# Cross attention with layer norm: the mask folded into keys and values, the softmax maximum taken from the score banks, and the splits of x on GpSimd

## The chip, the cores and the metric

The kernel runs on one core of one Trainium2 chip. The metric is the device time of one launch in microseconds; a median of three runs is given for the kernel before. The engines are TensorE (PE in the rows, its weight loads PEld), VectorE (DVE), ScalarE (ACT), GpSimd (POOL) and SyncE (SP), whose queue issues all DMAs of this kernel. They work through their own instruction lists in order and wait for each other by semaphores.

## What is computed

```python
qh = split(q @ wq.T + bq); kh = split(k @ wk.T + bk); vh = split(v @ wv.T + bv)
scores = einsum('ntd,nsd->nts', qh, kh) / sqrt(depth)
scores = scores + repeat(mask, h, axis=0)[:, None, :] * PAD      # PAD = -2**32 + 1
ctx = einsum('nts,nsd->ntd', softmax(scores), vh)
out = merge(ctx) + q
out = (out - mean) / sqrt(var + 1e-5) * gamma + beta
```

q is x (32 x 512 x 512), k and v are the context (32 x 77 x 512), all float32; there are 16 heads of depth 32. The mask is (32, 77). The repetition over heads pairs batch and head so that a head of a batch takes the mask row of a (head, parity of the batch) pair. A softmax row does not change when one number is added to all its scores.

## The kernel before

Float32 products are made of parts: each operand is split into a high part (rounded to fp32r by ScalarE) and a low part (the difference, by VectorE or GpSimd), and three products of parts are added in PSUM (`terms`). The sizes are P = 128, B = 32 batches, S = 77 keys, HEADS = 16, D = 512 in four groups of 128 columns (KC, NG).

Phase one (first block, lines 152 to 425) makes keys and values of all batches, in four chunks of 8 batches (CB), each of two halves of 4 batches (HB, HR = 308 columns). In a chunk TensorE makes 8 groups of key products (two halves of four `m`, 12 products each, L378) into the four banks `k_ps`, and then five value tiles (VT, L408, 12 products each) into four banks `v_ps`. ScalarE copies each key group with its bias to the high part in `k_out` (L277), VectorE makes the low part from the same bank (L322), and TensorE waits on `k_copied` before it writes a bank again. Value tiles get their bias from VectorE (L334). Tile j waits on `v_copied` of tile j - 4, so that its bank is free; in VectorE's list `values(c)` stands behind `low_keys_out(c, 1)`, and `low(c + 1)`, the low part of the next context (L314), stands between the two halves. On ScalarE `high(c + 1)` (L270) stands there likewise. SyncE stores keys and values to scratch tensors in DRAM and loads the next contexts. GpSimd clears `bd0` (L245), multiplies the mask by PAD (L251, two tensors `mask_pad` of 16 heads x 77), and makes the low parts of wq (L248) and of batch 0's x (L255).

Phase two (second block, from line 526) runs over the batches in steps `a`, each of eight small steps `s` = (h, t): half of the heads and a tile of 128 rows. In each, TensorE makes half of a q group (`q_half`, L612), the scores of 8 heads (`scores`, L628) into `s_ps[t % 2]`, transposes of probabilities (`turn`, L639) and the product with the values (`product`, L653), the latter two for earlier tiles. VectorE inverts the sums and scales the attention (L698, L710), adds the mask to the scores (`add_mask`, L787), takes the maximum of each head (`maximum`, L795), makes q's low part (L777), row statistics (L718, L722), and x's low part of batch a + 2 (`split_x`, L771). GpSimd subtracts the maximum (`subtract_max`, L898), adds the residual (L867), makes the row factors (L883, L885) and applies gamma and beta (L875, L878). ScalarE takes the exponential (L930), casts x to its high part (L940), copies q (L944) and the transposes (L950) and normalises (L954). The scores of a tile wait for `masked` of the tile two before. SyncE's list loads keys, then x of batch a + 2 behind `x_lo_ready` (L568), then values and rows, with the output stores between (L549). The last tile's subtraction is done by VectorE (`subtract_last_max`, L691).

## Time and profile before

| | |
|---|---|
| median of 3 runs | 1152.54 us (1152.19 to 1155.57) |
| the profiled execution | 1154.46 us |
| its span, first to last instruction | 1152.7 us |
| TensorE busy | 1121.0 us, 97% |
| VectorE busy | 931.6 us, 81% |
| GpSimd busy | 855.5 us, 74% |
| ScalarE busy | 614.9 us, 53% |

Phase one lasts to about 126 us, phase two to the end. Busy times are of instructions as the profiler saw them. A product's duration is longer than its distance to the next, since products overlap; distances of starts tell TensorE's pace. Granted clock 1.00 is TensorE's full 2.4 GHz, 0.5 is 1.2 GHz. In a row with an arrow in brackets the number is the idle time of that engine just before, and behind the arrow stands what ended it.

### The profile page before, as it was taken

What the parts mean: (1) busy time and instruction counts of PE and PEld (TensorE: products, weight loads), DVE (VectorE), ACT (ScalarE), POOL (GpSimd) and SP (SyncE); (2) the same over time, 40 slices, a digit from 0 to 9 for tenths busy, and PEclk for the clock granted to TensorE, in tenths of its full rate; (3) what the DMA queues carried; (4) which work ended last, traced back from release to release, by engine and by line L of the source; (5) the groups of instructions that cost most, each with busy time, mean ns of one, the idle gap of its engine ahead of it and who ended that gap; (6) DMA issues with size and microseconds to landing.
All of it is one profiled execution on the core that took longest, in us unless ns stands there. A gap on an engine that the chain in (4) does not pass through costs nothing.

```text
span 1152.7 us, 25667 instructions
## 1 busy us (share of the span) xinstructions
PE 1121.0 (97%) x7536; PEld 1036.7 (90%) x7536; DVE 931.6 (81%) x1677; ACT 614.9 (53%) x1003; POOL 855.5 (74%) x709
## 2 busy tenths in 40 slices
PE   7999899999999999999999999999999999999993
PEld 7888689999999999999999999999999999999983
DVE  5233578888888888888888988988888888988787
ACT  5221255555556655555555555665555565565551
POOL 1310235888888888888888888888888888888886
PEclk9999899999999999999999999999999999999997
DMA  8756233333333444433334333344434334333323
GB/s 252 273 188 238 73 89 89 89 109 96 117 119 116 126 126 126 126 116 119 92 112 120 97 113 120 117 126 126 126 117 124 109 90 123 109 106 115 89 80 130
DMA packets 145349, 141.98 MB, mean 123 GB/s; under 512 B 84868, under 2 KB 85892, under 8 KB 145316
## 3 DMA queue, kind: packets, MB, share of 16 engines
q1 hardware_dynamic: 145316, 141.55, 40.4%
q8 instruction: 19, 0.31, 0.1%
q14 instruction: 14, 0.11, 0.0%
HBM read 92.65 MB, written 48.85 MB: 123 GB/s over the span
## 4 chain that ended last, share of the span: by engine, by line
PE 83%; DVE 3%; POOL 1%; DMA 1%; ACT 0%; issue 0%; SPq 0%; DVEq 0%; POOLq 0%
PE q_ps L612 31%; PE o_ps L653 23%; PE s_ps L628 18%; PE t_ps L639 12%; DMA xT_raw<-in_xT 1%; POOL probs L898 0%; DVE stats L718 0%; DVE attn L749 0%; DVE row_max L795 0%; DVE probs L787 0%; DVE y L758 0%; PE q_ps L653 0%; POOL y L878 0%; POOL y L875 0%; SPq L558 0%
## 5 line engine op out<-in xcount | busy, mean ns | idle before, releaser
L898 POOL TENSOR_TENSOR probs<-probs,row_max 128x616 f32<-128x616 f32 x255 | 310.8, 1219 | 166.2 <-DVE row_max L795 166.1
L930 ACT ACTIVATE probs<-probs 128x616 f32<-128x616 f32 x256 | 183.3, 716 | 308.6 <-POOL probs L898 306.5
L653 PE MATMUL o_ps<-v_tiles,pt 128*128 128x66 f32 x2520 | 310.3, 270 | 2.6 <-DVE attn L710 2.6
L653 PEld LDWEIGHTS o_ps<-v_tiles,pt 128*128 128x128 f32 x2520 | 303.8, 192 | 3.1 <-issue 3.1
L628 PE MATMUL s_ps<-bd,q_hi 128*128 128x308 f32 x1024 | 261.4, 306 | 2.4 <-ACT q_hi L944 2.4
L787 DVE TENSOR_TENSOR probs<-s_ps,mask_pad 128x616 f32<-128x616 f32 x256 | 202.8, 792 | 51.9 <-PE s_ps L628 51.4
L612 PE MATMUL q_ps<-x_lo,wq_hi 128*128 128x512 f32 x500 | 218.3, 437 | 2.5 <-PEq L135 2.1
L795 DVE TENSOR_REDUCE row_max<-probs 128x8 f32<-128x616 f32 x256 | 202.3, 790 | 12.1
L612 PE MATMUL q_ps<-x_hi,wq_lo 128*128 128x512 f32 x500 | 197.9, 396 | 0.0
L612 PE MATMUL q_ps<-x_hi,wq_hi 128*128 128x512 f32 x500 | 197.6, 395 | 0.0
L628 PEld LDWEIGHTS s_ps<-bd,q_hi 128*128 128x128 f32 x1024 | 181.8, 189 | 14.3 <-ACT q_hi L944 2.8
L878 POOL TENSOR_TENSOR y<-y,beta_all 128x512 f32<-128x512 f32 x123 | 175.4, 1426 | 9.6
L950 ACT COPY pt<-t_ps 128x512 f32<-128x512 f32 (+1 forms) x320 | 172.8, 581 | 11.9 <-PE t_ps L639 11.9
L639 PE MATMUL t_ps<-ident,probs 128*128 128x128 f32 (+1 forms) x1280 | 171.8, 273 | 0.7 <-ACT pt L950 0.7
L875 POOL TENSOR_TENSOR y<-attn,gamma_all 128x512 f32<-128x512 f32 x123 | 163.7, 1331 | 4.3 <-ACT attn L954 4.3
L867 POOL TENSOR_TENSOR attn<-attn,x_rows 128x512 f32<-128x512 f32 x124 | 159.5, 1287 | 0.0
L628 PE MATMUL s_ps<-bd,q_lo 128*128 128x308 f32 x512 | 157.0, 307 | 0.0
L771 DVE TENSOR_TENSOR x_lo<-xT_raw,x_hi 128x512 fp32r<-128x512 f32 x124 | 144.8, 1170 | 13.8 <-ACT x_hi L940 13.4
L639 PEld LDWEIGHTS t_ps<-ident,probs 128*128 128x128 f32 (+1 forms) x1280 | 150.9, 139 | 2.1 <-ACT probs L930 0.9
L944 ACT ACTIVATE q_hi<-q_ps,bq_col 128x512 fp32r<-128x512 f32 x125 | 86.1, 689 | 84.9 <-PE q_ps L612 84.9
L710 DVE TENSOR_TENSOR attn<-o_ps,inv_sum 128x256 f32<-128x256 f32 x252 | 106.8, 424 | 17.9
L777 DVE SCALAR_TENSOR_TENSOR q_lo<-q_ps,bq_col,q_hi 128x512 fp32r<-128x512 f32 x125 | 93.3, 747 | 26.0 <-ACT q_hi L944 24.9
(82 smaller groups left out, 1276.8 us busy)
## 6 DMA issues: line engine op xcount, KB each, us to landing
xT_raw<-in_xT SPq DMA_DIRECT2D x32, 1024.0 KB, 5.7
x_rows<-in_x SPq DMA_DIRECT2D x32, 1024.0 KB, 5.7
out<-y SPq DMA_DIRECT2D x128, 256.0 KB, 2.1
k_scratch<-k_out SPq DMA_DIRECT2D x8, 1232.0 KB, 5.5
bd<-k_scratch SPq DMA_DIRECT2D x128, 77.0 KB, 2.4
v_scratch<-v_out SPq DMA_DIRECT2D x16, 264.0 KB
v_tiles<-v_scratch SPq DMA_DIRECT2D x256, 9.9 KB
ctx_raw<-in_ctxT SPq DMA_DIRECT2D x3, 1232.0 KB, 8.1
```

Source lines behind the costliest of these rows:

```text
L612: mm = pe.matmul(q_bank(b, g)[:, :], (wq_hi, wq_lo)[u][:, k, P * g:P * g + P], x_part[v][:, k, :], start=(k == 0 and n == 0), stop=(k == K ...
L628: mm = pe.matmul(s_ps[t % 2][:, j, 0:GS], (q_hi, q_lo)[u][:, g, P * t:P * t + P], bd[par][:, v, g, :, :].rearrange("p h s -> p (h s)"), st ...
L639: mm = pe.transpose(t_ps[(NT * h + i) % 2][0:w, P * t:P * t + P], probs[h][:, t, P * i:P * i + w], ident[:, :])
L653: mm = pe.matmul(bank_of(b, t)[:, col:col + tile_cols[i]], pt[h][0:w, i, P * t:P * t + P], v_tiles[v_buffer(b, h)][0:w, i, 0:tile_cols[i]] ...
L787: dve.tensor_tensor(probs[h][:, t, :].rearrange("p (j c) -> p j c", j=2), s_ps[t % 2][:, :, 0:GS], mask_pad[par][:, ROWS * h:ROWS * h + RO ...
L795: dve.tensor_reduce(row_max[:, u, :], probs[h][:, t, :].rearrange("p (h s) -> p h s", h=HH), AX.X, ALU.max).then_inc(max_ready, 1)
L867: pool.tensor_tensor(attn[par][:, t, :], attn[par][:, t, :], x_rows[:, t, :], ALU.add).then_inc(resid_done, 1)
L875: pool.tensor_tensor(y[par][:, t, :], attn[par][:, t, :], gamma_all[:], ALU.mult).then_inc(scaled, 1)
L878: pool.tensor_tensor(y[par][:, t, :], y[par][:, t, :], beta_all[:], ALU.add).then_inc(out_ready, 1)
L898: pool.tensor_tensor(v, v, row_max[:, u, :].unsqueeze(2).broadcast_to([P, HH, S]), ALU.subtract).then_inc(shifted, 1)
L930: act.activation(probs[h][:, t, :], probs[h][:, t, :], ACT.Exp).then_inc(exp_done, 1)
L950: act.copy(pt[h][0:w, i, :], t_ps[(NT * h + i) % 2][0:w, :]).then_inc(pt_ready, 1)
```

## The change

In phase one the mask becomes `keep` (1 for a kept key, 0 otherwise). Each key group gets bias and mask by VectorE (`centre_of_keys`) into a ring `k_part` of 6 slots, VectorE sums over the keys of a head, GpSimd multiplies the sum by -1/count and by `keep` and adds it (`centre_keys`), so that the kept keys of a head have mean zero and the others are zero; ScalarE copies the high part, VectorE makes the low part (`low_keys_out(n)`). Masked keys so have score zero. Values are multiplied by `keep_v` (GpSimd, `keep_values`), which is also written in the place of the ones that make the sums. `keep_v` comes from a small table, transposed by TensorE into `v_ps[3]` and copied by ScalarE in chunk 0. TensorE waits for `k_masked` and `v_biased` instead of `k_copied` and `v_copied`. The order of loads on SyncE, and of wq's and x's low parts on GpSimd, changes.

In phase two the mask addition is gone; VectorE takes the maximum from the score bank and subtracts it from the same bank; GpSimd does the splits of x instead of the subtractions. The core of the diff:

```diff
@@ phase one, sync
                 sp.dma_start(bk_col[:], bk).then_inc(bk_loaded, DMA)
+                mask_heads = mask.rearrange("(g q) i s -> q g (i s)", q=HG)
+                for q in range(HG):
+                    sp.dma_start(keep[DH * q:DH * q + DH, :, :, :].bitcast(I32).rearrange("p g i s -> p g (i s)"),
+                                 mask_heads[q].partition_broadcast(DH)).then_inc(mask_loaded, DMA)
+                sp.dma_start(keep_h[:].bitcast(I32), mask).then_inc(mask_loaded, DMA)
                 sp.dma_start(ctx_raw[:, :, HR:CR], ctx_src[:, :, 0, HR:CR]).then_inc(ctx_loaded, DMA)
...
-                for i in range(2):
-                    sp.dma_start(mask_pad[i][:].bitcast(I32), mask[i].partition_broadcast(P)).then_inc(mask_loaded, DMA)
                 for c in range(CHUNKS):
                     store_keys(c, 0)
-                    if 1 < c + 1 < CHUNKS:
-                        load(c + 1)
                     store_keys(c, 1)
+                    if c + 2 < CHUNKS:
+                        load(c + 2)
...
@@ phase one, gpsimd
+                pool.wait_ge(mask_loaded, (HG + 1) * DMA)
+                pool.tensor_scalar(keep[:], keep[:].bitcast(I32), 0, None, ALU.is_equal).then_inc(keep_set, 1)
+                pool.tensor_scalar(keep_h[:], keep_h[:].bitcast(I32), 0, None, ALU.is_equal).then_inc(keep_set, 1)
+                pool.wait_ge(count_step, 3)
+                pool.wait_ge(keep_set, 1)
+                pool.tensor_tensor(shift_of_key[:], keep[:], neg_rcount[:].unsqueeze(3).broadcast_to([P, NG, 2, S]),
+                                   ALU.mult).then_inc(keep_set, 1)
                 pool.memset(bd0[:].bitcast(F32), 0.0).then_inc(bd_zeroed, 1)
...
+                def centre_keys(c, half):
+                    for m in range(NG):
+                        n = (2 * c + half) * NG + m
+                        pool.wait_ge(k_summed, n + 1)
+                        at_least(pool, k_ready, n)
+                        pool.tensor_tensor(k_shift[:], shift_of_key[:, m, :, :].unsqueeze(1).broadcast_to([P, HB // 2, 2, S]),
+                                           k_sum[:, n % KS, :, :].unsqueeze(3).broadcast_to([P, HB // 2, 2, S]),
+                                           ALU.mult).then_inc(k_shift_ready, 1)
+                        pool.wait_ge(k_shift_ready, n + 1)
+                        pool.tensor_tensor(k_part[:, n % KS, :, :, :], k_part[:, n % KS, :, :, :], k_shift[:], ALU.add
+                                           ).then_inc(k_ready, 1)
+
+                def keep_values(c):
+                    if c == 0:
+                        pool.wait_ge(keep_v_ready, VT)
+                        for j in range(VT):
+                            pool.tensor_copy(v_out[0:v_n[j], j, :, DH], keep_v[0:v_n[j], j, :]).then_inc(ones_set, 1)
+                        pool.wait_ge(ones_set, VT)
+                    for j in range(VT):
+                        n = v_n[j]
+                        pool.wait_ge(v_biased, c * VT + j + 1)
+                        pool.tensor_tensor(v_out[0:n, j, :, 0:DH], v_out[0:n, j, :, 0:DH],
+                                           keep_v[0:n, j, :].unsqueeze(2).broadcast_to([n, HEADS, DH]),
+                                           ALU.mult).then_inc(v_copied, 1)
+
+                for c in range(CHUNKS):
+                    centre_keys(c, 0)
+                    centre_keys(c, 1)
+                    keep_values(c)
+                    if c == 1:
+                        pool.wait_ge(wq_hi_ready, 1)
+                        pool.tensor_tensor(wq_lo[:], w_raw[:], wq_hi[:], ALU.subtract).then_inc(wq_lo_ready, 1)
+                    if c == 2:
+                        pool.wait_ge(x_hi_ready, KC)
+                        for k in range(KC):
+                            pool.tensor_tensor(x_lo0[:, k, :], xT_raw[:, k, :], x_hi0[:, k, :], ALU.subtract
+                                               ).then_inc(x_lo_ready, 1)
...
@@ phase one, scalar
+                        act.wait_ge(k_ready, n + 1)
+                        act.copy(k_out[:, half * HB:half * HB + HB, 0, m, :],
+                                 k_part[:, n % KS, :, :, :].rearrange("p c i s -> p (c i) s")
+                                 ).then_inc(k_hi_copied, 1)
...
                     keys(c, 1)
                     if c == 0:
+                        act.wait_ge(keep_turned, 1)
+                        for j in range(VT):
+                            act.copy(keep_v[0:v_n[j], j, :], v_ps[3][0:v_n[j], HEADS * j:HEADS * j + HEADS]
+                                     ).then_inc(keep_v_ready, 1)
...
@@ phase one, vector
+                def centre_of_keys(n):
...
+                    dve.wait_ge(k_done, n + 1)
+                    at_least(dve, k_copied, n + 1 - KS)
+                    dve.scalar_tensor_tensor(out=k_part[:, slot, :, :, :].rearrange("p c i s -> p c (i s)"),
+                                             in0=k_ps[m][:, 0:HR].rearrange("p (c r) -> p c r", r=2 * S),
+                                             scalar=bk_sc[:, m:m + 1], in1=keep_of(m),
+                                             op0=ALU.add, op1=ALU.mult).then_inc(k_masked, 1)
+                    dve.wait_ge(k_masked, n + 1)
+                    dve.tensor_reduce(k_sum[:, slot, :, :], k_part[:, slot, :, :, :], AX.X, ALU.add
+                                      ).then_inc(k_summed, 1)
...
+                def keys(c, half):
+                    first = 2 * c * NG
+                    for n in range(first + half * NG, first + half * NG + NG):
+                        centre_of_keys(n)
+                        if half == 1:
+                            low_keys_out(n - NG)
+                    if half == 1:
+                        for n in range(first + NG, first + 2 * NG):
+                            low_keys_out(n)
...
+                low(0)
+                dve.wait_ge(keep_set, 2)
+                dve.tensor_reduce(neg_rcount[:], keep[:], AX.X, ALU.add).then_inc(count_step, 1)
...
+                keys(0, 0)
...
@@ phase one, tensor
-                            pe.wait_ge(k_copied, (2 * c + half - 1) * NG + m + 1)
+                            pe.wait_ge(k_masked, (2 * c + half - 1) * NG + m + 1)
...
+                        if (c, j) == (0, 3):
+                            pe.wait_ge(keep_v_ready, VT)
+                        at_least(pe, v_biased, c * VT + j - 3)
...
@@ phase two
-                    at_least(pe, masked, b * 8 + (4 * h + t - 1))
+                    at_least(pe, shifted, b * 8 + (4 * h + t - 1))
...
-                        if real(a):
-                            add_mask(a, h, t, par)
-                        if 4 <= s <= 6 and real(a + 2):
-                            split_x(a + 2, s - 3, par)
...
+                        if real(a):
+                            subtract_max(a, h, t)
...
@@ phase two, gpsimd
-                        if s == 0:
-                            if real(a - 1) and not is_last(a - 1):
-                                subtract_max(a - 1, 1, 3)
-                        elif real(a):
-                            subtract_max(a, (s - 1) // 4, (s - 1) % 4)
...
+                        if 3 <= s <= 6 and real(a + 2):
+                            split_x(a + 2, s - 3, par)
```

## Rows read from the trace of the kernel before

**Rows 1.** The page: span, busy time by engine, granted clock in 40 slices.
```profile
span 1152.7 us, 25667 instructions
...
PE 1121.0 (97%) x7536; PEld 1036.7 (90%) x7536; DVE 931.6 (81%) x1677; ACT 614.9 (53%) x1003; POOL 855.5 (74%) x709
...
PEclk9999899999999999999999999999999999999997
```
**Rows 2.** Stretches: from:to, length, busy by engine (instructions), clock, DMA.
```profile
120.00:140.00 20.00, 16.58 (x73) 13.49 (x71) 9.88 (x14) 6.76 (x11) 7.21 (x8) 0.91 0.33 84
...
400.00:600.00 200.00, 200.00 (x1379) 185.95 (x1378) 174.50 (x323) 115.01 (x189) 171.61 (x142) 1.00 0.39 113
1100.00:1153.00 53.00, 31.77 (x239) 29.83 (x237) 40.89 (x80) 18.16 (x29) 39.41 (x32) 0.85 0.31 110
```
**Rows 3.** Timeline of phase one: start us, duration us, engine, line.
```profile
4.98 0.43 SPq L163 DMA_DIRECT2D ctx_raw<-in_ctxT  x1
...
10.36 1.22 ACT L270 CAST ctx_hi<-ctx_raw 128x1232 fp32r<-128x1232 f32 x1 [1.17 <-DMA ctx_raw<-in_ctxT]
...
15.25 0.38 PE L378 MATMUL k_ps<-ctx_lo,wk_hi 128*128 128x308 f32 x1
...
20.79 2.26 ACT L270 CAST ctx_hi<-ctx_raw 128x2464 fp32r<-128x2464 f32 x1 [3.23 <-DMA ctx_raw<-in_ctxT]
...
22.13 0.40 PE L408 MATMUL v_ps<-wv_lo,ctx_hi 128*128 128x512 f32 x1
...
23.18 2.73 DVE L314 TENSOR_TENSOR ctx_lo<-ctx_raw,ctx_hi 128x2464 fp32r<-128x2464 f32 x1 [3.30 <-ACT ctx_hi L270]
...
36.10 0.30 PE L378 MATMUL k_ps<-ctx_lo,wk_hi 128*128 128x308 f32 x1
```
**Rows 4.** Groups of phase two: count, then busy us, mean ns, idle before.
```profile
L898 POOL TENSOR_TENSOR probs<-probs,row_max 128x616 f32<-128x616 f32 x255 | 310.8, 1219 | 166.2 <-DVE row_max L795 166.1
...
L787 DVE TENSOR_TENSOR probs<-s_ps,mask_pad 128x616 f32<-128x616 f32 x256 | 202.8, 792 | 51.9 <-PE s_ps L628 51.4
...
L795 DVE TENSOR_REDUCE row_max<-probs 128x8 f32<-128x616 f32 x256 | 202.3, 790 | 12.1
```
**Rows 5.** The same view: groups of phase one, and phase two's first memset.
```profile
L322 DVE SCALAR_TENSOR_TENSOR k_out<-k_ps,bk_sc,k_out 128x308 fp32r<-128x308 f32 x32 | 16.1, 535 | 21.3 <-ACT k_out L277 21.3
...
L251 POOL TENSOR_SCALAR mask_pad<-mask_pad 128x1232 f32<-128x1232 int32 x2 | 6.6, 3334 | 0.0
...
L255 POOL TENSOR_TENSOR x_lo<-xT_raw,x_hi 128x512 fp32r<-128x512 f32 x4 | 5.1, 1301 | 20.5 <-ACT x_hi L301 20.5
...
L248 POOL TENSOR_TENSOR wq_lo<-w_raw,wq_hi 128x2048 fp32r<-128x2048 f32 x1 | 4.6, 4639 | 23.5 <-ACT wq_hi L297 23.5
...
L887 POOL MEMSET bd<- 128x2464 f32 x1 | 2.2, 2155 | 62.2 <-POOLq L135 62.2
...
L345 DVE TENSOR_TENSOR ctx_lo<-ctx_raw,ctx_hi 128x308 fp32r<-128x308 f32 x4 | 1.9, 472 | 0.0
```
**Rows 6.** L771 alone (ns min/median/max), and two groups of GpSimd.
```profile
L771 DVE TENSOR_TENSOR x_lo<-xT_raw,x_hi x124: 679/1239/1836, 126.9 to 1055.9; 128x512 fp32r<-128x512 f32 x124
...
L878 POOL TENSOR_TENSOR y<-y,beta_all 128x512 f32<-128x512 f32 x123 | 175.4, 1426 | 9.6
...
L867 POOL TENSOR_TENSOR attn<-attn,x_rows 128x512 f32<-128x512 f32 x124 | 159.5, 1287 | 0.0
```
**Rows 7.** Timeline of the start of phase two.
```profile
126.51 0.47 PE L612 MATMUL q_ps<-x_lo,wq_hi 128*128 128x512 f32 x1 [2.09 <-PEq L135]
...
127.46 0.63 PE L612 MATMUL q_ps<-x_lo,wq_hi 128*128 128x512 f32 x1
...
132.79 0.41 SPq L568 DMA_DIRECT2D xT_raw<-in_xT  x1
...
141.02 0.59 PE L628 MATMUL s_ps<-bd,q_hi 128*128 128x308 f32 x1 [2.35 <-ACT q_hi L944]
```
**Rows 8.** Timeline of the last batch, VectorE.
```profile
1119.81 1.48 DVE L691 TENSOR_TENSOR probs<-probs,row_max 128x616 f32<-128x616 f32 x1
```

155 lines of the change are left out of this document (78 added, 77 removed).

## The prediction

> **What bounds the kernel now.** The page first: TensorE is busy for 1121 of 1152.7 us, VectorE for 932 and GpSimd for 856 [rows 1]. The reader is to see that no other engine is full, and from the table of stretches that between 400 and 600 us TensorE is busy for all 200.00, at the full granted clock, with VectorE at 174.5 and GpSimd at 171.6 [rows 2]. So in the steady loop of phase two only TensorE's own work counts, and the change takes none of it away. What can move is where TensorE stands still: the first microseconds, the passage between the phases (3.4 us idle in 120:140) and the last 53 us, of which it works 31.8 [rows 2]. Phase one is bound by TensorE too: a group of key products takes (22.13 - 15.25) / 4 = 1.72 us and a value tile (36.10 - 22.13) / 5 = 2.79, one directly behind the other [rows 3]. There VectorE, ScalarE and GpSimd have slack. The question is whether what the change puts there still fits.
>
> **Phase two, steady loop.** Per batch GpSimd loses 8 subtractions of 1.22 and gets 4 splits of 1.30 [rows 4, 5]: 4.6 us less. VectorE loses 8 mask additions of 0.79 and 4 splits of about 1.2, and gets 8 subtractions [rows 4, 6]. Before has no subtraction that reads PSUM and a broadcast; the mask addition has the same size, one PSUM and one SBUF input, and I take its 0.79, as I take 0.79 for the maximum read from PSUM. Its bounds are 0.7 and 1.0; at 1.0 VectorE would have 8 x 2 x 0.21 = 3.4 us more, still no more than the splits leave. The scores of step u now wait for `shifted` of u-2 (before: `masked`), which comes one maximum later, 0.8 us, where two steps of about 3.9 us lie between. Everything is hidden behind TensorE: 0 us. Worth without this cover: some 4 us a batch. SyncE's load of xT waits for the splits; on GpSimd the last one falls in its step 6 and the load is issued a step and a half later, behind an output store: hidden too.
>
> **Start of phase two.** The phase starts at 126.2. GpSimd begins with a memset of 2.2 us and three of about 0.5, to 129.8, and only then splits x of batch 1: 4 x 1.30, to 135.0 [rows 5]. VectorE did this beside the memsets. SyncE's next xT load waits for that split; it was issued at 132.79, now at 135.1: +2.3. ScalarE's cast of this load stands ahead of the q copy for which TensorE waited 2.35 us at 141.02 [rows 7]. **+2.3** (0 if TensorE arrives later anyway, +3.2 if the clock stays low longer).
>
> **End.** In the last batch VectorE's extra subtraction of 1.48 goes [rows 8] (the one that takes the mask's place is already counted), and GpSimd's subtractions no longer stand between maximum and exponential. Next in line are the attention scalings, in VectorE's order, and they move with it: **-2.0** (-1 to -9, the latter if four times 1.22 and the holds of rows 6 were all on the path).
>
> **Phase one, the new chain.** A key group was: products, ScalarE copy, VectorE difference. Now it is: VectorE bias and mask (0.54, as L322), VectorE sum (0.47: half of the 616-element reduction), GpSimd multiply and add, ScalarE copy (0.5; four times as many elements took 1.22 [rows 3]), VectorE low part (0.47) [rows 4, 5]. TensorE waits for the first of these only. GpSimd's pass is not in the trace. From 512 elements in 1.30 and 2048 in 4.64 an element costs 2.18 ns and the start 0.18: 0.85 for the add of 308; the multiply with broadcasts by L898 0.65; with 0.07 of semaphore each, **1.65** a pass [rows 4, 5]. Bounds 1.45 and 1.9. In second halves VectorE's low parts read two SBUF tensors beside GpSimd; L771, which did, took 0.68 to 1.84 (median 1.24), and L878 1.43 where L867 took 1.29 [rows 6], so I take 1.9 a pass there.
> The trace shows such instructions stretched by about half a microsecond. The Trainium skill has a rule for it (SBUF — State Buffer, who interferes with whom): a VectorE instruction with two SBUF inputs and a GpSimd instruction lock each other out for a whole instruction. The spread of L771 agrees. By the rule at its strictest each low part would wait 0.85, and the forecast would be some 6 us higher.
>
> **First stall.** Five mask loads are issued ahead of the second half of context 0 (0.43 and a gap each [rows 3]), 2.4 us: ScalarE's cast starts between 10.36 (if that issue was early enough anyway) and 12.8; I take 12.0, nearer to the full delay, since this load was waited for, and VectorE's low part of it ends at 14.75. GpSimd's mask compare is half of L251, 1.7, and a small one, 0.5, from a landing at about 11: 13.2 [rows 5]. Then VectorE counts: 0.79 + 0.31 + three small ones of 0.17 + 0.79, with gaps to 17.3, and the first bias and mask at 17.9. TensorE is through at 15.1 and waits **2.8**. Idle stretches of 2.1 and 2.35 us were each followed by half clock (products of 0.63 instead of 0.40; granted mean 0.91 over 20 us, so 1.7 us lost) [rows 2, 7]: **+1.7**. Five mask transposes: **+0.5**.
>
> **Second stall: value tile 3 of chunk 0.** It waits for ScalarE's copies of the mask, which stand behind `keys(0,1)`. GpSimd's multiply of mask and count ends at 18.6, its memset at 20.0 (2.2 moved from the start into the chain); four passes 26.6; ScalarE copy 27.2, cast of context 1 (2.26) 29.5; VectorE low part (2.73) 32.2 [rows 3]; bias, mask, sum 33.3; four passes at 1.9 40.9; copy 41.4; five small copies, an estimate of 0.25 each, 42.6. TensorE arrives at 17.9 + 1.7 + 6.8 + 0.5 + 3 x 2.79 = 35.3: **+7.3 and +1.7** of clock.
>
> **Value tile 4 of chunk 1.** It needs the bias on tile 0, which on VectorE stands behind all of `keys(1,1)`. From the chunk's start: 6.8 (four groups) + 1.1 + 1.65 + 0.5 + 2.3 + 2.7 + 1.1 + 4 x 1.9 + 0.5 + 0.5 + 0.7 = 25.45; TensorE arrives at 13.6 + 11.15 = 24.75: **+0.8**.
>
> **Chunk 2, the same tile.** Ahead of the first pass GpSimd has the value masks of chunk 1 (to 3.2 into the chunk) and wq's low part (4.64 [rows 5]), to 7.9. Then 4 x 1.65 + 0.5 + 2.3 + 2.7 = 20.0, and + 1.1 + 7.6 + 1.7 = 30.4 against 24.75: **+5.7 and +1.7**. Chunk 3 has no next context to split; its bias comes at 23 against 24.75: 0.
> Phase one: 2.8 + 1.7 + 0.5 + 7.3 + 1.7 + 0.8 + 5.7 + 1.7 = **+22.2**.
>
> **Sum.** 22.2 + 2.3 - 2.0 = 22.5. The profiled execution took 1154.46 (span 1152.7 and 1.8 around it), so 1177.0 against it. It lies 1.9 above the median of 1152.54; against that 1175.0, which I forecast.
>
> **The rivals.**
> A: light passes. Pass 1.45, no holds, clock kept: the same recurrence gives +11 to +13 in phase one; with the start and end as above 1165. Chance 0.25. For it: slack in every queue that I read coarsely.
> B: heavy passes. 1.9 everywhere and holds: the wait of chunk 1 grows to 2.4 and costs a clock stretch too, phase one +29 to +32: 1183. Chance 0.15.
> C: nothing measurable. The mask is ready before TensorE needs it, tile 3 finds its bank free, and the end gives what the start costs: 1149.1 to 1156.0. That needs passes short enough that GpSimd is never asked after, and the chain through `keys(0,0)`, two ScalarE and two VectorE instructions is over 10 us without them. Chance 0.06.
> D: faster. Its place is the last 53 us, where TensorE idles 21 [rows 2]: the four subtractions, 1.48 and the stretched instructions, about 9 us, all on the path. It decides only if phase one costs under 5.5, that is the first stall alone: 5.0 - 9 + 0 = 1148.5. Chance 0.04.
> E: the steady loop stalls, because splits on GpSimd hold back xT each batch: 1 us x 30 on top, 1205. Against it: the order above, with GpSimd 4.6 us a batch lighter. Chance 0.04.
>
> **How the numbers follow.** The forecast itself has 0.46 (A 0.25, B 0.15, the rest 0.14). Its own range 1169 to 1181 comes from a pass 0.1 longer or shorter (about 2 us each) and the landing of the masks (1 us). With A and B the range is 1162 to 1186; C, D and E, 0.14, are left out. A measurement of this kernel can tell 0.3%, 3.5 us, from no change: faster 0.04 (D), same 0.06 (C), slower 0.90.
>
> **What would show it.** The table of stretches: TensorE under 20.00 near 15, 40 and 100 us, granted clock falling behind each. The waits: TensorE on VectorE's k_part, on ScalarE's keep_v, on VectorE's v_out. The last product of phase one near 146 instead of 124. 400:600 still full. I would be wrong if a pass takes far from 1.65, if idle near 40 us leaves no low clock, or if the loop of phase two has a wait of TensorE.

## The result, and the profile after

The changed kernel takes 1177.98 us (median of 4 runs, 1177.65 to 1178.07) against 1153.19 (4 runs, 1152.19 to 1155.57): a recorded ratio of 1.0203, interval 1.0191 to 1.0215 (the two medians by themselves divide to 1.0215). It is slower by 25 us; whether that is more than 2% the interval leaves open. The forecast was 1175.0 with a range of 1162 to 1186. The profiled execution has a span of 1176.1 us where before had 1152.7 [rows 1]: 23.4 more, of which the sum had foreseen 22.5.

The page first (span, busy time and share of each engine, granted clock in 40 slices):

```profile
span 1176.1 us, 25445 instructions
...
PE 1127.1 (96%) x7541; PEld 1040.7 (88%) x7541; DVE 823.9 (70%) x1622; ACT 612.8 (52%) x1008; POOL 761.6 (65%) x667
...
PEclk9899989999999999999999999999999999999997
```

VectorE and GpSimd have lost 108 and 94 us of work against [rows 1], and the kernel is slower. Whoever reads busy time alone would have forecast a gain. TensorE is busy for 6 us more, with five more instructions, the mask transposes: nearly all of it is half clock. The second and the sixth slice show 8. The sixth is the start of phase two, which before shows in its fifth; the second is new.

Stretches of after (from:to, length, then busy time of each engine with its instructions, granted clock, DMA share, GB/s):

```profile
0.00:20.00 20.00, 11.38 (x57) 11.19 (x58) 10.64 (x23) 8.28 (x11) 6.59 (x10) 0.93 0.82 253
20.00:40.00 20.00, 14.93 (x82) 12.75 (x80) 11.04 (x14) 4.86 (x7) 12.31 (x14) 0.93 0.26 87
40.00:60.00 20.00, 16.19 (x86) 14.41 (x87) 11.26 (x19) 4.42 (x11) 13.59 (x21) 0.80 0.88 308
...
100.00:120.00 20.00, 15.68 (x80) 13.11 (x79) 14.38 (x25) 1.81 (x4) 16.17 (x17) 0.91 0.52 192
...
400.00:600.00 200.00, 200.00 (x1384) 186.07 (x1384) 144.54 (x296) 115.49 (x191) 135.36 (x116) 1.00 0.38 118
```

The last line answers to the middle one of [rows 2]: TensorE is full as before, at full clock, and VectorE and GpSimd have shrunk from 174.5 and 171.6 to 144.5 and 135.4. All of that is hidden. The holes are in phase one, near 17, 40 and 105 us. Who leaves them (TensorE's waits; total, times, longest):

```profile
PE v_ps L512 <- ACT keep_v L354: 8.9, 1, 8.9
PE k_ps L473 <- DVE ctx_lo L428: 5.8, 1, 5.8
PE v_ps L512 <- DVE v_out L417: 5.0, 2, 4.3
PE s_ps L730 <- ACT q_hi L1020: 3.6, 1, 3.6
PE q_ps L714 <- PEq L142: 3.0, 1, 3.0
PE k_ps L473 <- DVE k_part L383: 2.8, 1, 2.8
```

5.8 us is the wait for the first loads, which before had too. The first, third and last are the waits that the prediction names in phase one. Four products mark the stages, here three of them in before (the fourth is in [rows 7]), then all in after (timeline: start, duration, engine, line; idle before it in brackets):

```profile
118.66 0.39 PE L422 MATMUL k_ps<-x_lo,wq_hi 128*128 128x512 f32 x1
...
152.97 0.47 PE L612 MATMUL q_ps<-x_lo,wq_hi 128*128 128x512 f32 x1 [0.37 <-DVE q_lo L777]
...
1103.57 0.48 PE L612 MATMUL q_ps<-x_lo,wq_hi 128*128 128x512 f32 x1
```
```profile
140.89 0.39 PE L526 MATMUL k_ps<-x_lo,wq_hi 128*128 128x512 f32 x1
...
149.68 0.47 PE L714 MATMUL q_ps<-x_lo,wq_hi 128*128 128x512 f32 x1 [3.03 <-PEq L142]
...
178.19 0.47 PE L714 MATMUL q_ps<-x_lo,wq_hi 128*128 128x512 f32 x1 [0.38 <-DVE q_lo L865]
...
1128.85 0.48 PE L714 MATMUL q_ps<-x_lo,wq_hi 128*128 128x512 f32 x1
```

The first of each is the start of batch 0's q products at the end of phase one, the next-to-last a product with the same short wait early in phase two, the last the last batch's last q half. With the first product of phase two (126.51 before, [rows 7]) the 23.4 us divide so:

| stretch | before | after | difference | forecast |
|---|---|---|---|---|
| to the q products | 118.66 | 140.89 | +22.2 | +22.2 |
| from there to the first product of phase two | 7.85 | 8.79 | +0.9 | 0 |
| from there to the product after the q_lo wait | 26.46 | 28.51 | +2.05 | +2.3 |
| from there to the last q half | 950.60 | 950.66 | +0.06 | 0 |
| from there to the end | 49.13 | 47.25 | -1.9 | -2.0 |

### The profile page after: what moved, and what is told of

Its sections match the earlier page's. It is cut to its first block, busy times and chain, and to the rows that moved or that the text cites. A ratio compares the mean times of both kernels' runs of the same rounds, so it can differ in the third digit from the quotient of the medians.

```text
span 1176.1 us, 25445 instructions
## 1 busy us (share of the span) xinstructions
PE 1127.1 (96%) x7541; PEld 1040.7 (88%) x7541; DVE 823.9 (70%) x1622; ACT 612.8 (52%) x1008; POOL 761.6 (65%) x667
## 4 chain that ended last, share of the span: by engine, by line
PE 83%; DVE 2%; POOL 1%; issue 0%; DMA 0%; ACT 0%; DVEq 0%; SPq 0%; POOLq 0%
PE q_ps L714 31%; PE o_ps L755 22%; PE s_ps L730 18%; PE t_ps L741 12%; DMA xT_raw<-in_xT 0%; POOL x_lo L981 0%; DVE stats L812 0%; DVE attn L843 0%; DVE y L852 0%; PE q_ps L755 0%; DVE attn L804 0%; DVE row_max L875 0%; ACT q_hi L1020 0%; DVE y L858 0%; DVE y L833 0%
## 5 line engine op out<-in xcount | busy, mean ns | idle before, releaser
L875 DVE TENSOR_REDUCE row_max<-s_ps 128x8 f32<-128x616 f32 x256 | 203.4, 795 | 120.5 <-PE s_ps L730 120.4
L981 POOL TENSOR_TENSOR x_lo<-xT_raw,x_hi 128x512 fp32r<-128x512 f32 x124 | 159.1, 1284 | 122.5 <-ACT x_hi L1016 122.4
L884 DVE TENSOR_TENSOR probs<-s_ps,row_max 128x616 f32<-128x616 f32 x256 | 204.7, 799 | 5.7
L959 POOL TENSOR_TENSOR y<-attn,gamma_all 128x512 f32<-128x512 f32 x123 | 158.4, 1288 | 12.4 <-ACT attn L1030 12.4
L962 POOL TENSOR_TENSOR y<-y,beta_all 128x512 f32<-128x512 f32 x123 | 158.4, 1288 | 9.7
L714 PEld LDWEIGHTS q_ps<-x_hi,wq_hi 128*128 128x128 f32 x500 | 94.2, 188 | 22.6
```

The lines of the kernel that those rows point to most:

```text
L714: mm = pe.matmul(q_bank(b, g)[:, :], (wq_hi, wq_lo)[u][:, k, P * g:P * g + P], x_part[v][:, k, :], start=(k == 0 and n == 0), stop=(k == K ...
L875: dve.tensor_reduce(row_max[:, u, :].rearrange("p (j h) -> p j h", j=2), score_heads(t), AX.X, ALU.max).then_inc(max_ready, 1)
L884: dve.tensor_tensor(probs[h][:, t, :].rearrange("p (j h s) -> p j h s", j=2, s=S), score_heads(t), row_max[:, u, :].rearrange("p (j h) -> ...
L959: pool.tensor_tensor(y[par][:, t, :], attn[par][:, t, :], gamma_all[:], ALU.mult).then_inc(scaled, 1)
L962: pool.tensor_tensor(y[par][:, t, :], y[par][:, t, :], beta_all[:], ALU.add).then_inc(out_ready, 1)
L981: pool.tensor_tensor(x_lo[par][:, k, :], xT_raw[:, k, :], x_hi[par][:, k, :], ALU.subtract).then_inc(x_lo_ready, 1)
```

## The experiments

The theory: the whole loss is order in phase one. No engine there is too slow; TensorE waits because single short instructions stand behind long chains on GpSimd, ScalarE and VectorE. The rivals: the passes on GpSimd (a pass is its multiply and add for one key group) are themselves too much; phase two has its own cost; stalls cost twice, for the clock falls after each. Each kernel is compared by span and stages of its profile, and by the ratio of its runs to those of before on the same chip.

### Phase two alone

Phase one of before, phase two of after; the mask is then left out of the computation.

> Phase one of the kernel before, phase two of the changed one; the mask is left out of the scores, so it computes the attention without a mask. Theory (phase two alone: start +2, steady loop 0, end -1.9): span 1152 to 1153.5, the wait for ScalarE's q copy near 15 us into phase two 3.6 instead of 2.4, the loop of phase two without a TensorE wait. Rival (the new phase two costs or gains in the loop): over 3 us away from the kernel before, either side.

Measured: 1155.71 us, ratio 1.001 [1.0, 1.002]; span 1153.9, 1.2 above before and 0.4 above the top of what was expected. TensorE is full from 400 to 600. The longest wait is where it should be, and longer:

```profile
125.88 0.47 PE L610 MATMUL q_ps<-x_lo,wq_hi 128*128 128x512 f32 x1 [2.09 <-PEq L135]
...
142.28 0.60 PE L626 MATMUL s_ps<-bd,q_hi 128*128 128x308 f32 x1 [5.78 <-ACT q_hi L916]
...
154.49 0.47 PE L610 MATMUL q_ps<-x_lo,wq_hi 128*128 128x512 f32 x1 [0.37 <-DVE q_lo L761]
```

From the phase's first product to the product after the q_lo wait it takes 28.6 us, before 26.5, after 28.5. So the start of phase two costs 2.1 whatever phase one does. The wait is longer than the 3.6 expected mainly because TensorE came to it 1.5 us sooner: here no half clock followed the passage. Loop and end together (1153.9 less 154.49) gave back 0.3, not 1.9, and phase one happened to be 0.6 shorter. The 22 us are of phase one.

### The next context ahead of the key copies

```diff
-                    keys(c, 0)
                     if c + 1 < CHUNKS:
                         high(c + 1)
+                    keys(c, 0)
```

> The changed kernel with ScalarE's cast of the next context moved ahead of its copies of the first half's keys, nothing else. Theory (the order of the queues: GpSimd's passes hold up the cast, the cast holds VectorE's low part, that holds all bias and mask work of the second half): the wait for keep_v falls from 8.9 to about 2.3 us with less time at half clock, the waits of value tile 4 in chunks 1 and 2 (0.7 and 4.3) go, span about 14 us shorter, 1162. Rival (GpSimd's throughput, 8 passes of 1.8 and the value masks a chunk, is the limit whatever the order): the waits stay within 2 us, span 1174 to 1176.

Measured: 1167.98 us, ratio 1.012 [1.0103, 1.0137]; span 1165.0, that is 11.1 less than after, where 14 were expected. The tile-4 waits are gone but for 0.2 us. The wait on keep_v fell to 6.2 instead of 2.3, and the timeline has the reason:

```profile
20.37 2.28 DVE L450 TENSOR_TENSOR wv_lo<-w_raw,wv_hi 128x2048 fp32r<-128x2048 f32 x1
20.55 2.81 POOL L286 TENSOR_TENSOR k_part<-k_part,k_shift 128x308 f32<-128x308 f32 x1
22.60 3.34 DVE L374 TENSOR_TENSOR ctx_lo<-ctx_raw,ctx_hi 128x2464 fp32r<-128x2464 f32 x1
23.50 3.00 POOL L282 TENSOR_TENSOR k_shift<-shift_of_key,k_sum 128x308 f32<-128x308 f32 x1
26.58 0.85 POOL L286 TENSOR_TENSOR k_part<-k_part,k_shift 128x308 f32<-128x308 f32 x1
```

L286 is 0.85 alone. It ran for 2.81 while VectorE's L450 of 2.28 was on, and L282 (0.70 alone) for 3.00 beside L374. Each GpSimd instruction ends 0.6 to 0.7 us, about its own duration, behind the VectorE one that began before it: 23.36 against 20.37 + 2.28 = 22.65, and 26.50 against 22.60 + 3.34 = 25.94. Of the order most came back; two such meetings, 2 us and 2.3 us, took the rest. From 19.77 to 38.57 GpSimd now goes from one instruction to the next without a longer pause, so for this one wait its throughput has become the limit, as the rival has it.

### VectorE's long subtraction cut in four

```diff
-                dve.tensor_tensor(wv_lo[:], w_raw[:], wv_hi[:], ALU.subtract).then_inc(wv_lo_ready, 1)
+                for k in range(KC):
+                    dve.tensor_tensor(wv_lo[:, k, :], w_raw[:, k, :], wv_hi[:, k, :], ALU.subtract
+                                      ).then_inc(wv_lo_ready, 1)
```

> VectorE makes the low part of wv, one subtraction of 2.3 us with two SBUF inputs, in four subtractions of a quarter of it each. Theory (the first GpSimd addition took 2.83 us instead of 0.85 because it had to wait for the end of the VectorE instruction that began before it): it now waits for a quarter only, takes 1.4 or less, and the chain to the wait on keep_v is 1.4 shorter: wait 8.9 to 7.5, span 1176.1 to 1174.7. Rival (the two only share bandwidth, or the first execution of that form is slow in itself): the first addition stays near 2.8, and the span stays within 0.5.

Measured, in the timeline:

```profile
20.78 4.30 DVE L451 TENSOR_TENSOR wv_lo<-w_raw,wv_hi 128x512 fp32r<-128x512 f32 x4
20.97 1.20 POOL L286 TENSOR_TENSOR k_part<-k_part,k_shift 128x308 f32<-128x308 f32 x1
22.30 0.97 POOL L282 TENSOR_TENSOR k_shift<-shift_of_key,k_sum 128x308 f32<-128x308 f32 x1
23.36 1.17 POOL L286 TENSOR_TENSOR k_part<-k_part,k_shift 128x308 f32<-128x308 f32 x1
```

The addition takes 1.20 instead of 2.83, the four quarters together 4.30 instead of 2.28: the two engines took turns, one instruction each. That fits a hold for a whole instruction and not a shared bandwidth. The wait on keep_v is 7.9 (8.9) and ends at 43.04 instead of 43.81, 0.8 earlier against 1.4 expected: the other quarters held GpSimd three more times. The q products start at 139.59, 1.3 earlier than in after; most of the rest is a shorter stretch at half clock. The span is 1174.4, but the medians hardly move (1177.91, ratio 1.0197 [1.018, 1.0214]), and in the run with the splits of batch 1 below, whose phase one is that of after, the q products start 1.2 later than in after. So the hold is shown; that its microsecond reaches the end is not. The Trainium skill (SBUF — State Buffer, who interferes with whom) has this rule, and adds that what decides is who issues first; both meetings above agree, since VectorE began first in each.

### keep_v early

The transposes of the mask stand in TensorE's first stall, and ScalarE's copies right behind its cast of wv:

```diff
                 act.copy(wv_hi[:], w_raw[:]).then_inc(wv_hi_ready, 1)
+                act.wait_ge(keep_turned, 1)
+                for j in range(VT):
+                    act.copy(keep_v[0:v_n[j], j, :], v_ps[3][0:v_n[j], HEADS * j:HEADS * j + HEADS]
+                             ).then_inc(keep_v_ready, 1)
```

> The changed kernel with the five mask transposes in the first stall and ScalarE's copies of them ahead of its key copies. Theory: the wait of tile 3 for keep_v goes, but tile 4 finds its bank's bias behind keys(0,1) on VectorE and waits about 7 us there; the transposes' 0.4 us are hidden; in all 2 to 3 us less, span about 1173.5. Rival (the copies of keep_v are the cause by themselves): 9 us less and the half clock after it too, 1165.

Measured: 1174.75 us, ratio 1.0186 [1.0159, 1.0212]. The wait on keep_v is gone, and the one that stands in the table is

```profile
43.98 0.75 PE L512 MATMUL v_ps<-wv_lo,ctx_hi 128*104 128x512 f32 x1 [8.81 <-DVE v_out L417]
```

TensorE stands as long one tile later, for the bias of tile 0, which on VectorE waits for the same GpSimd passes. The q products start at 138.60, 2.3 earlier, as expected, and not 8.9. The span is 1170.0, 3.5 below what was expected, but not by this mend: 2.2 of its 6.1 us came at the start of phase two and 1.7 behind the last q half, where the clock stood better in this execution (the median run was 2.9 longer). Taking a wait away here only showed the next one in the same shadow.

### The first stall filled

Where TensorE waits for the first bias and mask:

```diff
+                for i in range(19):
+                    pe.matmul(v_ps[0][:, 0:HR], wk_hi[:, 0, 0:P], ctx_hi[0][:, 0, 0:HR], start=True, stop=True)
```

> The changed kernel with 19 products of 308 columns into a free bank, 2.7 us of work that nobody reads, in the first stall of TensorE (2.8 us). Theory (idle time brings the half clock, which costs 1.6 us on top of the wait): the wait at 17.6 us goes to about 0, the second half of keys runs at full clock from its start, but the wait for keep_v, which other engines set, swallows it: its end stays at 43.8 and the span is unchanged within 0.5 us. Rival (the half clock comes anyway): the products after 17.6 still take 0.46 us, span unchanged or longer.

Measured: 1177.93 us, ratio 1.0219 [1.0194, 1.0245]; span 1174.9.

```profile
17.69 0.38 PE L473 MATMUL k_ps<-ctx_lo,wk_hi 128*128 128x308 f32 x1 [0.35 <-DVE k_part L383]
43.83 0.80 PE L514 MATMUL v_ps<-wv_lo,ctx_hi 128*128 128x512 f32 x1 [10.15 <-ACT keep_v L354]
```

There is no half clock behind the place of the first stall, and TensorE only waits 10.2 instead of 8.9 for keep_v, to the same 43.8. So the first stall and its clock, 4.5 us in the sum, are worth nothing by themselves: they lie in the shadow of the keep_v chain. That it was the filling that kept the clock up is not shown: in three other runs the stall stood open (2.95, 3.18 and 2.41 us: next context first, splits of batch 1, tile 4 alone) and the granted clock was 1.00 over the first 20 us all the same. The q products start at 140.55, 0.3 earlier; of the 1.2 us that the span is shorter, the rest came in phase two and says nothing of the stall.

### The value biases ahead of the late low parts

```diff
-                    if half == 1:
-                        for n in range(first + NG, first + 2 * NG):
-                            low_keys_out(n)
...
                                           ALU.add).then_inc(v_biased, 1)
+                        if j < NG:
+                            low_keys_out((2 * c + 1) * NG + j)
```

> In VectorE's list of each chunk of phase one the low parts of the second half's four key groups, which wait for GpSimd's passes and ScalarE's copies, no longer stand ahead of the biases of the value tiles: one follows behind each of the first four biases. Nothing else changes. Theory (value tile 4 waits only because the bias on tile 0 stands behind these low parts): its waits of 0.7 us in chunk 1 and 4.3 in chunk 2 go, and the half clock behind the second of them (1.7), so the span falls by 6.7, from 1176.1 to about 1169.4; the wait on keep_v of 8.9 stays as it is. Rival (GpSimd itself is too late, by wq's low part of 4.6 us in chunk 2): the wait moves on, to the products of chunk 3 that wait for a context part or for a key bank, and the span falls by 2 at most.

Measured: 1177.28 us, ratio 1.0186 [1.0169, 1.0203]. The q products start at 136.43, 4.5 earlier; in chunk 2 1.5 us of the wait stayed. But the span is 1176.7, where 1169.4 was expected. Most of the gain, 3.7 us, is lost at once in the passage between the phases (a further 1.5 in the last 30 us, by the clock):

```profile
148.96 0.77 PE L713 MATMUL q_ps<-x_lo,wq_hi 128*128 128x512 f32 x1 [6.77 <-PEq L142]
```

6.8 us instead of 3.0, where SyncE waits 7.2 us for the last store of values to land (5.5 in after, 1.9 in before). Neither theory had seen this. The next kernel has the same edit with `c < CHUNKS - 1` beside `j < NG`, and the last chunk keeps its old order.

> The changed kernel with one mend alone: in chunks 0 to 2, not in the last, the value biases stand ahead of the low parts of the second half. With all four chunks so, phase one was 4.5 us shorter, and the passage 3.7 longer. Theory (the two are separate): the 4.5 stay, the passage is 3.0 again, and the span is 1176.1 - 4.5 = about 1171.6, up to 1.7 more if half clock falls otherwise in the last 30 us. Rival (the 4.5 were only moved: the stores of the last chunk are late because GpSimd is behind from chunk 2 on): passage above 5.5 and span above 1174.

Measured: the q products start at 135.83, 5.1 earlier, the passage has 4.34 idle, the span is 1171.7 (1171.6 expected); 1175.40 us in the median, ratio 1.018 [1.0163, 1.0197]. Most of the passage came back, though not all: 3.0 was expected. The agreement of the spans is closer than it should be, for the profiled execution was 1.9 faster than the median one.

### The splits of batch 1 on VectorE

```diff
-                        if 3 <= s <= 6 and real(a + 2):
+                        if 3 <= s <= 6 and real(a + 2) and not (isinstance(a, int) and a == -1):
                             split_x(a + 2, s - 3, par)
```

and at the head of VectorE's list of phase two

```diff
+                for k in range(KC):
+                    dve.wait_ge(x_hi_ready, 4 + k + 1)
+                    dve.tensor_tensor(x_lo[1][:, k, :], xT_raw[:, k, :], x_hi[1][:, k, :], ALU.subtract
+                                      ).then_inc(x_lo_ready, 1)
```

> Of all splits of x in phase two, those of batch 1 alone are back on VectorE, at the head of its list; they stand behind GpSimd's memsets no more. Theory: xT of batch 2 is issued 2 us earlier, TensorE's third and fourth waits come back to those of the kernel before, the 2.05 us of the start of phase two go, and the span falls from 1176.1 to about 1174. Rival (the load lands hardly earlier, since other loads share its queues then): 0.5 or less.

Measured: from the first product of phase two (150.84) to that after the q_lo wait (177.17) 26.3 us, in after 28.5, in before 26.5: the 2.05 us are gone, as the theory has it. The rival has a part: the load is issued 2.2 us earlier than in after, counted from the phase's first product, but ScalarE's cast of it starts only 1.5 earlier, and the wait on the q copy is 2.11 instead of 3.58. The span does not show it (1176.7; 1177.78 us, ratio 1.0194 [1.0177, 1.0211]). In this execution phase one took 1.2 more, and half clock in the last 30 us held twice as long as in after (a product of 2.34 instead of 1.75 behind the 2.5 us wait there), 1.6 more.

### All mends together

The edits above (next context first, keep_v early, biases first, splits of batch 1), and two more: `act.dma_start` in place of `sp.dma_start` for the five mask loads, ahead of ScalarE's first instruction, with VectorE's counts ahead of `low(0)`; and GpSimd's list with

```diff
+                pool.memset(bd0[:].bitcast(F32), 0.0).then_inc(bd_zeroed, 1)
                 pool.wait_ge(mask_loaded, (HG + 1) * DMA)
...
-                pool.memset(bd0[:].bitcast(F32), 0.0).then_inc(bd_zeroed, 1)
```

> Six mends in one, none of which touches the arithmetic: the mask loads issued from ScalarE's queue at the start and counted by VectorE ahead of its low part of context 0; the memset of bd0 at the head of GpSimd's list; the cast of the next context ahead of the key copies; the transposes of the mask in TensorE's first stall and their copies behind the cast of wv; the biases of value tiles ahead of the low parts of the second half; the splits of batch 1 on VectorE. Theory (the whole loss was order, and hidden work costs nothing): phase one costs 0.5 for the transposes and 0 to 1 beside it, the passage 0.95, the start of phase two 0, the end gives 1.9: span 1152.7 + 0.5 + 0.5 + 0.95 - 1.9 = about 1152.8, which no measurement here tells from the kernel before. Rival (GpSimd's eight passes per chunk, stretched beside VectorE, are themselves too long, so a wait stays in some chunk and half clock with it): span 1157 to 1162.

Measured: 1157.62 us, ratio 1.0019 [1.001, 1.0029], span 1157.3. That is 4.5 above the theory's span and inside the rival's range, so the number alone would speak for the rival. The waits do not. In phase one no wait of TensorE is left but the one for the first loads:

```profile
PE k_ps L472 <- DVE ctx_lo L427: 7.2, 1, 7.2
PE q_ps L713 <- PEq L142: 6.9, 1, 6.9
```

and in its stretches (columns as above):

```profile
20.00:40.00 20.00, 20.00 (x105) 17.07 (x104) 17.97 (x24) 7.48 (x10) 18.59 (x22) 1.00 0.49 165
```

GpSimd works 18.6 us of 20 there, and TensorE does not notice. With all passes in place the q products start at 120.51 against 118.66 in before. The rival, that the passes are too long in themselves, has fallen. The 4.6 us against before divide into 1.9 to the q products, 4.8 in the passage, -1.8 at the start of phase two and -0.3 at the end. Two things are left: 1.4 us at the start and 6.9 of idle in the passage. The next kernel takes the biases-first edit back in the last chunk (`c < CHUNKS - 1`, as above).

> As the run with all mends, except that in the last chunk of phase one the low parts of the second half stand ahead of the value biases again, as in the changed kernel. The run with all mends had no wait of TensorE in phase one, but a passage of 6.9 us instead of 3.0. Theory (in the last chunk the mend delayed the key store, behind which SyncE's xT load and five value stores are queued, so that all landed together at the end): key store and xT load are issued about 4 us earlier, the passage falls to about 3.0 and the span by 3.9, from 1157.3 to 1153.4. Rival (the value stores are late for GpSimd's masks alone, which come after the last product in any order): passage 6 or more, span above 1156.

Measured: span 1153.5 (1153.4 expected), 1153.54 us, ratio 0.9992 [0.998, 1.0004]. What changed is when SyncE gets to its stores, with all mends, then with the last chunk as it was:

```profile
119.57 0.38 SPq L199 DMA_DIRECT2D k_scratch<-k_out  x1
120.06 0.45 SPq L244 DMA_DIRECT2D xT_raw<-in_xT  x1
120.55 4.37 SPq L216 DMA_DIRECT2D v_scratch<-v_out  x5
```
```profile
116.30 0.38 SPq L199 DMA_DIRECT2D k_scratch<-k_out  x1
116.79 0.45 SPq L244 DMA_DIRECT2D xT_raw<-in_xT  x1
118.03 4.58 SPq L216 DMA_DIRECT2D v_scratch<-v_out  x5
```

The key store comes 3.3 us earlier and the first value store 2.5; the idle of the passage is 3.96 instead of 6.88. In before the key store was issued at 106.08, 12.6 us ahead of the q products, now it is 3.9 ahead. That fits with a passage that still costs 1.9 more than before's 2.09; a version with earlier stores was not tried. The next kernel moves four of the mask loads behind ScalarE's first cast; the diff is of that alone, its other moves are in the expectation:

```diff
                     act.copy(ctx_hi[0][:, k, 0:HR], ctx_raw[:, k, 0:HR]).then_inc(start_hi_ready, 1)
+                    if k == 0:
+                        for q in range(HG):
+                            act.dma_start(keep[DH * q:DH * q + DH, :, :, :].bitcast(I32).rearrange("p g i s -> p g (i s)"),
+                                          mask_heads[q].partition_broadcast(DH)).then_inc(mask_loaded, DMA)
```

> As the run before it, with the masks moved: four of the five mask loads are issued by ScalarE behind its first two instructions instead of ahead of its table load, the fifth by SyncE behind the second half of context 0; VectorE makes its low part of context 0 first, counts the mask next, and makes the rows for the transposes last; the transposes stand ahead of value tile 1. In the run with all mends the first product began at 7.2 us instead of 5.8, because the table load and the first loads came later. Theory: first product back at 5.9, no stall near 15, keep_v ready before 31, and the span 1.3 below the run before it, about 1152.1: less than the 1152.7 of the kernel before, but not by what a measurement tells. Rival (the masks land later and TensorE waits for the first bias or for keep_v by as much): the same span as the run before it, or more, with that wait in the table.

Measured: span 1151.4 (1152.1 expected), 1153.29 us, ratio 0.9996 [0.9984, 1.0007]. First product at 5.9 as expected; but TensorE stood 2.5 us at 17.0, which was not. No half clock followed it, and none followed the 2.5 us wait of the last 30 us, so this execution has fewer low stretches than most; the medians of this kernel and the one before it differ by 0.3 us. The last kernel goes after the 2.5 us (again one of its edits; VectorE's counts go ahead of its low part of context 0 too):

```diff
-                pool.wait_ge(mask_loaded, (HG + 1) * DMA)
+                pool.wait_ge(mask_loaded, HG * DMA)
```

> As the run with the masks moved later, except that GpSimd's first comparison waits for the four loads of keep alone, no longer for that of keep_h too (12.8 us in that run), and VectorE counts the mask ahead of its low part of context 0, which waits for a landing of its own. In that run TensorE stood 2.5 us at 17.0 for the first bias and mask (L385 at 16.36, behind the low part from 13.85 to 15.29 and the counts to 16.4). Theory: comparison from about 11.5 to 13.3, counts to 14.4, low part to 15.9, first bias and mask at 15.9, the stall about 2.0 instead of 2.5, and if the comparison ends before 13 the counts are through when the cast lands: stall 1.2. Span 1150.2 to 1151, below the kernel before by 1.7 to 2.5 (0.15 to 0.2%). Rival (the loads of keep land with the others at 12.5, since all share the queues): stall 2.5 or more, span as in that run, 1151.4 or 1153 if the clock falls after it.

Measured: the stall is 1.1 (1.2 expected in the better case) and the q products start 0.3 earlier, at 120.72. Yet the span is 1155.9, where 1150.2 to 1151 was expected, and the median 1155.74, ratio 1.0002 [0.9992, 1.0011]. From the phase's first product to the q_lo wait it is 26.1 us instead of 24.6, and the product in the last 30 us took 2.37 instead of 1.30. In both places the clock was lower for longer in this execution. The half microsecond won is below what this kernel can show. None of the last three versions can be told from before, so none beats it.

## Point by point

**Steady loop, 0.** Right: 0.06 over 950 us. The two unknown prices came out at the value taken, in the groups of 400 to 600 us (count, busy us, mean ns, idle before):

```profile
L875 DVE TENSOR_REDUCE row_max<-s_ps 128x8 f32<-128x616 f32 x52 | 41.3, 795 | 23.5 <-PE s_ps L730 23.5
L884 DVE TENSOR_TENSOR probs<-s_ps,row_max 128x616 f32<-128x616 f32 x51 | 40.8, 799 | 1.1
...
L981 POOL TENSOR_TENSOR x_lo<-xT_raw,x_hi 128x512 fp32r<-128x512 f32 x25 | 32.1, 1283 | 22.0 <-ACT x_hi L1016 22.0
```

0.79 was taken for the first two, 1.30 for the third.

**End, -2.0.** Right in this profile: -1.9. But the clock leaves the value open. All 13 runs with the new phase two have the same end, and from the last q half on it took 45.6 us in two of them, 47.2 to 47.3 in five, after among them, and 48.5 to 48.9 in six; before, of which there is one profile, took 49.13. They differ behind the 2.5 us wait: TensorE came to its next wait 4.4, 6.0 or 7.3 to 7.6 us later. So the end gave between 0.2 and 3.5 us, and that after's execution fell on the middle size is luck. Before's own stretch there was 6.0, as after's.

**Start of phase two, +2.3.** Right in the total, +2.05, and in its cause: the run with the splits of batch 1 on VectorE took it away. Its rows:

```profile
153.02 5.05 POOL L981 TENSOR_TENSOR x_lo<-xT_raw,x_hi 128x512 fp32r<-128x512 f32 x4
...
158.14 0.41 SPq L670 DMA_DIRECT2D xT_raw<-in_xT  x1
...
165.40 0.60 PE L730 MATMUL s_ps<-bd,q_hi 128*128 128x308 f32 x1 [3.58 <-ACT q_hi L1020]
```

The load is issued 8.46 us behind the first product of the phase, before 6.28 [rows 7]: 2.2 later, as worked out. But the prediction put the whole delay into the wait, and the wait grew by 1.2 only, from 2.35 to 3.58: ScalarE's cast of the load started 5.2 us behind the issue instead of 6.1. The other 0.8 came behind the wait, where half clock held longer than in before. The sum had named a clock cost only as its upper bound, so that the two parts make 2.05 is in part luck.

**Phase one, +22.2.** The total is exact, by terms that are not all exact. From the timeline of after:

```profile
20.17 0.70 POOL L282 TENSOR_TENSOR k_shift<-shift_of_key,k_sum 128x308 f32<-128x308 f32 x1
20.77 2.28 DVE L450 TENSOR_TENSOR wv_lo<-w_raw,wv_hi 128x2048 fp32r<-128x2048 f32 x1
20.95 2.83 POOL L286 TENSOR_TENSOR k_part<-k_part,k_shift 128x308 f32<-128x308 f32 x1
...
43.30 0.46 ACT L354 COPY keep_v<-v_ps 128x16 f32<-128x16 f32 x5
...
43.81 0.80 PE L512 MATMUL v_ps<-wv_lo,ctx_hi 128*128 128x512 f32 x1 [8.88 <-ACT keep_v L354]
```

- *First stall*, 2.8 forecast, 2.8 measured, with half clock behind it that cost 1.4 instead of 1.7. But it is not worth what the sum gave it: see the run that filled it.
- *A pass*: 0.70 + 0.85 with its gaps is 1.77 from start to start in first halves (1.65 taken) and 1.81 in second halves (1.9 taken). The hold beside VectorE's low parts was paid by VectorE: L396 takes 0.47 alone and 0.93 beside GpSimd.
- *Second stall*, 7.3 forecast, 8.9 measured. keep_v was ready at 43.8 instead of 42.6. Missed: the meeting of the first addition with wv_lo, 2.0 us. The prediction knew the rule and used it for the low parts alone; it never asked what else of VectorE reads two SBUF tensors in that time. On the other side the five copies took 0.46 together instead of 1.25. The half clock lasted from 37.6 to 47.8 and cost tile 3 1.9 instead of 1.7 (4.72 us from its start to that of tile 4, against 2.79).
- *Tile 4 of chunk 1*, 0.8 forecast, 0.7 measured.
- *Tile 4 of chunk 2*, 5.7 forecast, 4.3 measured, and 1.6 of clock, 1.7 forecast. The chunk starts at 79.7. GpSimd was through with the value masks of chunk 1 at 2.2 behind that, not at 3.2, and with wq_lo at 6.8 (81.94 + 4.61), not 7.9; TensorE arrived 0.2 later than reckoned. The rest of the chain ran as worked out.

By starts of products: up to value tile 0 of chunk 0 (26.29, before 22.13 [rows 3]) 4.2 us were lost, 5.0 forecast (TensorE came to the first stall some 0.5 sooner than in before, and the clock cost 0.3 less). From there to tile 4 of that chunk (48.53) it took 22.2 where four tiles take 11.2: 11.1 lost, 9.0 forecast. The remaining 7.0 of the 22.2 stand against 8.2. So the errors are -0.8, +2.1 and -1.2. That they cancel is luck; the range of 1169 to 1181 was the real size of what the sum could know.

**The passage, 0 forecast, +0.9 measured.** The sum has no term for this stage, and gives no reason for leaving it out. The prediction followed GpSimd's value masks to the biases and to TensorE, not to the stores. The last store waits for a mask of 1.05 us that before did not have, and its landing ends the phase.

**The rivals.** A (light passes) and B (heavy) differ from the forecast mainly in the length of a pass; it is 1.77 to 1.81, between. C and D needed phase one to cost next to nothing. It can, as the mended kernels show, but not in the order of this change; and D's 9 us at the end were 1.9, in no run more than 3.5. E needed a wait in the loop, and there is none.

## What to carry to other kernels

When work moves onto an engine with slack, the slack of the whole run says nothing; write out that engine's list for one stage and ask for each single instruction what stands ahead of it, then do the same on the engine that takes over from it. Of several stalls in the shadow of one chain only the one that ends last counts, so fill or remove that one first, and expect its neighbour to appear in the same place. The kernel stood 24.8 us above before, median against median; with six mends it stood 2.6 above the before runs measured beside it. The four of them that were run alone took 11.0, 4.2, 2.6 and 2.1 off by the same reckoning, each to within some 2 to 3 us. That is too coarse to rank the small ones or to say that the mends help each other; only the stages of the profiles do the first. A step that delays a store must be followed to the end of its phase, even where no engine waits for the store.

## What the runs showed of the hardware

- A VectorE instruction that reads two SBUF tensors and a GpSimd instruction that reads SBUF do not run at the same time: an addition of 0.85 us became 2.83, and with the VectorE instruction in quarters 1.20. With one of VectorE's two inputs in PSUM nothing of this was seen. L884 of after (score bank and row_max) has the same size as the subtraction L898 [rows 4], runs beside GpSimd for the whole loop, and took 798 to 801 ns in 256 cases, where L771 [rows 6] took 679 to 1836. That is not because row_max is small: before's mask addition reads the score bank and 616 elements of SBUF beside a busier GpSimd, and its 256 times are as narrow:

```profile
L884 DVE TENSOR_TENSOR probs<-s_ps,row_max x256: 798/799/801, 154.5 to 1143.4; 128x616 f32<-128x616 f32 x128
...
L787 DVE TENSOR_TENSOR probs<-s_ps,mask_pad x256: 779/790/800, 130.5 to 1118.1; 128x616 f32<-128x616 f32 x128
```

- The other side of the same: GpSimd's L962 is L878 of before [rows 6], unchanged in the program. Its mean fell from 1426 to 1288 ns (the median from 1298 to 1283), most likely because VectorE's splits, with two SBUF inputs, are gone from the loop; that was not tested by itself.
- GpSimd multiplies two broadcast operands of 308 elements in 0.70 us and adds two plain ones in 0.85. So broadcasting made nothing slower here; a multiply of plain operands was not run.
- A stall of TensorE is not always followed by half clock (1.2 instead of 2.4 GHz). In after the first stall of phase one, 2.78 us of idle, had the next product at 0.60 instead of 0.38. After 2.41 us (value biases first) and 1.97 (VectorE's subtraction in four) the clock fell about a microsecond behind the stall. After 2.95 (next context first), 3.18 (splits of batch 1 on VectorE), 2.41 (tile 4 alone) and 2.47 (masks later) it did not, and the granted clock was 1.00 over the first 20 us. What sets this was not tested. It makes single executions differ where the program is the same: by 1.2 us to the q products (after and the run with the splits of batch 1), by up to 3.3 us behind the last q half. The three stretches of phase one in after cost 1.4, 1.9 and 1.6 us; a term of 1.7 for each stall is an estimate, not a law.
- Five loads issued from ScalarE ahead of its table load moved the first product from 5.8 to 7.2 us: the issues took 2.3 us of ScalarE, and its table load of 1.28 began at 3.13 instead of 0.75. The table load was not the last thing waited for: ScalarE's first instruction behind it started at 5.31 instead of 3.94, 0.89 us behind its end, when a part of the context landed. So the first loads landed later too; the two causes were not tested apart.
